# Attention with relative shift and sign MLP on one core: values of a unit in one block, a new table of jobs, and the output product summed in PSUM under the transposed layers

## The chip, the core and the metric

The kernel runs on one core of a Trainium2 chip. A time is the device time of one execution in microseconds (us); lower is better. All matrix engines, vector engines and queues named below belong to that one core: PE (TensorE), DVE (VectorE), ACT (ScalarE), POOL (GpSimd) and the DMA queue that SP (SyncE) feeds.

## What is computed

The input x is 16 batches of 512 rows of 128 numbers, float32. With xn the layernorm of x:

```
out = x + attention(xn) + mlp(xn)

attention:  y = layernorm(xn) * g + b
            q, k, v = y @ Wq + bq, y @ Wk + bk, y @ Wv + bv     # 16 heads of 8
            p = pe @ Wp                                         # positions, 512 rows
            s = (q + u) . k  +  relative_shift((q + v_bias) . p)
            head = softmax(s / sqrt(8)) @ v
            return head @ Wo + bo

mlp:        h = [xn, -xn];  h = relu(s0 * h @ sign(k0)) * 2
            h = relu(s1 * h @ sign(k1)) * 2;  return s2 * h @ sign(k2)   # 512, 512, 128 wide
```

The relative shift is done by writing a unit's 512x512 position scores to memory with rows of 513 and reading them back with rows of 512.

## The kernel before

**Units and halves.** A unit is one head of one batch: 256 units in all, numbered u. The program is written out as a list of halves (`HALVES`), two to a unit, 32 to a batch, and every engine's part walks through the same halves in the same order. In a half PE does, in this order:

1. two blocks of position scores (`positions`, L838, into the two banks of `ps_pos`) and two blocks of content scores (`content`, L850, into the two banks of `ps_con`), interleaved; the content of a unit comes `2*CONTENT_LAG` = 12 halves after its positions;
2. `turn` (L862): eight 128x128 transposes of finished scores into the two banks of `ps_pt`, 17 halves after the unit's positions;
3. the half's entry in the table of jobs, if it has one (`do_job`); all jobs share one bank, `ps_job`;
4. `values` (L876): products of the exponentials of half a unit with v (and a column of ones), into `ps_av`, eight matmuls in the program and 16 on the engine (two passes each), one half after their transposes.

**The other engines in a half.** ACT copies the positions to `pos_sb` (L509), takes the exponential of the transposed scores into `pt_sb` (L523), and then evicts the job (L478 to L495). DVE adds shifted positions to contents and takes the row maximum (L682, twice), subtracts it (L690, twice, with its own job between the two), and evicts the jobs V, TO, WO and TY. POOL splits evicted layers into a high and a low part in place (L397, L401 for q and k, L413, L416 for the MLP and the layernormed rows), four instructions a split. SP issues a write of 1 MB (L331) and a read of 1 MB (L341) for each unit: the write when its four position blocks lie in `pos_sb`, the read right behind the write that is two units later.

**Who waits for whom.** Content block 0 or 1 of a half needs its bank of `ps_con` free, which is the L682 of the half before. `turn` needs `ps_pt` free, which is the exponential of the half before. A job needs the job before it evicted from `ps_job`. `values` needs its exponential. The exponential overwrites `pt_sb`, which has four rows of 512 (`N_PT`), so it waits for the values one half back.

**The table.** `FRONT`, `MIDDLE` and `BACK` give each batch's jobs as (half, name, number): half 0 of a batch is where the positions of its first unit start, negative halves lie in the batch before, and numbers over 31 in the one after; `EARLY` and `END` are the same for the first and the last batch. A batch has T1, TZ (transposes of the two normalised inputs), QG and KG (four groups each of q and k), V, L0 and L1 (four blocks each of the first two layers), L2, TO (transposes of four groups of head outputs), TH (transposes of the assembled heads), WO (the output product, `w_sb["o"]` as weights, 512 rows at once) and TY (four transposes of the sum `y_t` of layers and attention). L1 and L2 have eight matmuls and are spread over two halves, four in each.

## Time and profile before

| | us |
|---|---|
| median of 3 runs | 1446.93 |
| lowest and highest of them | 1445.94, 1519.36 |
| the profiled execution | 1446.42 |
| its span in the trace | 1444.6 |

| engine | busy in the span |
|---|---|
| PE | 1434.1 us, 99% |
| DVE | 1337.1 us, 93% |
| ACT | 1226.2 us, 85% |
| POOL | 858.2 us, 59% |
| DMA, mean of 16 engines | 97.2% by the main queue, 381 GB/s |

Busy time of PE is modelled and includes the flight of a matmul through the array, so it overstates how near PE is to its peak. The granted TensorE clock is 0.9 or more of full speed in every slice of the span.

### The profile page before, as it was taken

The page shows a single profiled execution, that of the slowest core. Times are in us where ns is not written, and L with a number is a line of the kernel's source. Part 1 is how long each engine was busy: PE and PEld are TensorE (multiplying, and loading weights), DVE is VectorE, ACT ScalarE, POOL GpSimd, SP SyncE. Part 2 cuts the span into 40 slices and gives each one's busy share as a digit, 9 for nine tenths or more (in the row PEclk, how much of TensorE's full clock was granted, in tenths as well). Part 3 has the DMA queues.
Part 4 walks back from the last instruction along what each step waited for, and adds up shares of the span by engine and source line. Part 5 has one row for each costly group of instructions (what it writes and reads, how often), then busy time and mean ns, then how long its engine had stood idle before and what let it go on. Part 6 is the DMA issues. An engine that isn't in the chain of part 4 may idle for free.

```text
span 1444.6 us, 42221 instructions
## 1 busy us (share of the span) xinstructions
PE 1434.1 (99%) x16170; PEld 972.3 (67%) x16170; DVE 1337.1 (93%) x3489; ACT 1226.2 (85%) x1365; POOL 858.2 (59%) x1321
## 2 busy tenths in 40 slices
PE   8999999999999999999999999999999999999999
PEld 4666666666676666666666676666766666676666
DVE  6799999999999999999999999999999999999996
ACT  5688888888888898898888888888888888888874
POOL 5676565666665676565765666566565766654510
PEclk9999999999999999999999999999999999999999
DMA  5999999999999999999999999999999999999992
GB/s 202 356 403 409 392 402 390 387 401 383 408 388 390 396 380 408 386 397 395 383 411 378 408 385 391 401 386 405 382 393 402 386 400 390 398 382 392 394 398 105
DMA packets 80872, 550.45 MB, mean 381 GB/s; under 512 B 9376, under 2 KB 10528, under 8 KB 15136
## 3 DMA queue, kind: packets, MB, share of 16 engines
q1 hardware_dynamic: 80240, 547.06, 97.2%
q8 instruction: 129, 2.11, 0.6%
q10 hardware_dynamic: 432, 0.69, 0.2%
q14 instruction: 71, 0.58, 0.1%
HBM read 274.57 MB, written 273.15 MB: 379 GB/s over the span
## 4 chain that ended last, share of the span: by engine, by line
PE 96%; DVE 1%; DMA 1%; ACT 1%; issue 0%; POOL 0%; SPq 0%; POOLq 0%
PE ps_pt L862 36%; PE ps_av L876 19%; PE ps_pos L838 15%; PE ps_job L765 12%; PE ps_job L729 4%; PE ps_job L719 3%; PE ps_job L744 2%; PE ps_job L752 1%; PE ps_job L740 1%; PE ps_job L735 1%; DMA sc_sb<-shift 1%; PE ps_con L850 1%; ACT pt_sb L523 1%; DVE sc_sb L682 0%; PE ps_job L746 0%; PE ps_job L748 0%
## 5 line engine op out<-in xcount | busy, mean ns | idle before, releaser
L682 DVE CUSTOM_DVE_ANT_0 sc_sb<-ps_con,sc_sb 128x512 f32<-128x512 f32 x1024 | 662.0, 682 | 76.7 <-PE ps_con L850 68.2
L509 ACT COPY pos_sb<-ps_pos 128x1024 f32<-128x1024 f32 x510 | 518.3, 1016 | 177.9 <-PE ps_pos L838 170.9
L690 DVE TENSOR_SCALAR sc_sb<-sc_sb,nmax 128x512 f32<-128x512 f32 x1024 | 611.6, 629 | 0.1
L862 PE MATMUL ps_pt<-c_sb,sc_sb 128*128 128x128 f32 x4048 | 553.5, 280 | 1.8 <-ACT pt_sb L523 0.7
L523 ACT ACTIVATE pt_sb<-ps_pt 128x1024 f32<-128x1024 f32 x506 | 519.2, 1026 | 13.3 <-PE ps_pt L862 13.3
L862 PEld LDWEIGHTS ps_pt<-c_sb,sc_sb 128*128 128x128 f32 x4048 | 433.9, 141 | 126.6 <-issue 99.4
L876 PE MATMUL ps_av<-pt_sb,v_sb 128*9 128x128 f32 x8192 | 319.9, 274 | 0.1
L876 PEld LDWEIGHTS ps_av<-pt_sb,v_sb 128*9 128x9 f32 x8192 | 172.7, 90 | 184.3 <-issue 182.1
L413 POOL CAST h<-act_sb 128x256 fp32r<-128x256 f32 x256 | 97.6, 410 | 303.8 <-ACT act_sb L492 296.4
L850 PE MATMUL ps_con<-k_stack,q_stack 26*128 26x512 f32 x1024 | 261.1, 496 | 1.1 <-DVE nmax L682 1.0
L838 PE MATMUL ps_pos<-p_stack,q_stack 26*128 26x512 f32 x1024 | 259.8, 496 | 1.0 <-ACT pos_sb L509 0.7
L416 POOL TENSOR_TENSOR h<-act_sb,h 128x256 fp32r<-128x256 f32 x256 | 201.0, 806 | 0.0
L765 PE MATMUL ps_job<-h,w 128*128 128x512 f32 x640 | 189.6, 418 | 0.0
L838 PEld LDWEIGHTS ps_pos<-p_stack,q_stack 26*128 26x128 f32 x1024 | 97.2, 181 | 116.7 <-issue 111.7
L397 POOL TENSOR_TENSOR k_stack<-act_sb,c_sb 128x256 fp32r<-128x256 f32 x126 | 75.0, 616 | 100.0 <-ACT act_sb L487 96.3
L765 PEld LDWEIGHTS ps_job<-h,w 128*128 128x128 f32 x640 | 109.1, 190 | 15.1 <-issue 0.2
L397 POOL TENSOR_TENSOR q_stack<-act_sb,c_sb 128x256 fp32r<-128x256 f32 x124 | 73.4, 612 | 51.3 <-ACT act_sb L487 43.2
L401 POOL TENSOR_TENSOR q_stack<-act_sb,q_stack 128x256 fp32r<-128x256 f32 x124 | 102.1, 844 | 0.0
L850 PEld LDWEIGHTS ps_con<-k_stack,q_stack 26*128 26x128 f32 x1024 | 97.9, 181 | 5.4 <-DVE nmax L682 4.2
L401 POOL TENSOR_TENSOR k_stack<-act_sb,k_stack 128x256 fp32r<-128x256 f32 x126 | 101.2, 824 | 0.0
L492 ACT ACTIVATE act_sb<-ps_job,col 128x512 f32<-128x512 f32 x128 | 87.7, 685 | 0.6 <-PE ps_job L765 0.5
L682 DVE DVE_READ_ACCUMULATOR2_ANT nmax<- 128x1 f32 x1024 | 81.9, 80 | 0.0
(116 smaller groups left out, 1024.1 us busy)
## 6 DMA issues: line engine op xcount, KB each, us to landing
shift<-pos_sb SPq DMA_DIRECT2D x256, 1026.0 KB, 8.2
sc_sb<-shift SPq DMA_DIRECT2D x256, 1024.0 KB, 10.2
x_sb<-in_x SPq DMA_DIRECT2D x16, 256.0 KB, 10.6
out<-x_sb SPq DMA_DIRECT2D x15, 256.0 KB, 10.6
c_sb<-in_consts ACTq DMA_DIRECT2D x1, 288.0 KB, 7.4
sc_sb<-in_wp SPq DMA_DIRECT2D x1, 256.0 KB, 4.3
sc_sb<-in_stack_w ACTq DMA_DIRECT2D x1, 256.0 KB, 5.2
heads<-in_pe_t SPq DMA_DIRECT2D x1, 256.0 KB, 6.3
```

Of the source, the lines that this page charges most:

```text
L397: pool.tensor_tensor(dst[:, cut], src[:, cut], low.broadcast_to([P, S // len(CUTS)]), ALU.mult) \
L401: last = pool.tensor_tensor(dst[:, cut], src[:, cut], dst[:, cut].bitcast(F32), ALU.subtract)
L416: last = pool.tensor_tensor(dst[:, 1, cut], src[:, cut], dst[:, 0, cut].bitcast(F32), ALU.subtract)
L509: act.copy(to, ps_pos[:, :, :]).then_inc(s_pe, 1)
L523: act.activation(pt_sb[:, 2 * i:2 * i + 2, :], pt_banks(k)[:, :, :], ACT.Exp, scale=-1.0) \
L682: dve.tensor_tensor_reduce(sc_sb[:, m % N_SC, t, :], ps_con[:, k, :], sc_sb[:, m % N_SC, t, :], -SCALE, 3.4e38, ALU.add, ALU.min, nmax[:, ...
L690: dve.tensor_scalar(sc_sb[:, m % N_SC, t, :], sc_sb[:, m % N_SC, t, :], nmax[:, m % N_SC, t:t + 1], None, ALU.subtract).then_inc(s_sub, 1)
L765: return pe.matmul(ps_job[:, :], lhs, src[:, a, hl, :], start=(a == 0 and hl == 0), stop=(a == len(before) - 1 and hl == 1))
L838: ins = pe.matmul(ps_pos[:, bank, :], QS[rows, g, t * P:(t + 1) * P], PS[rows, g, :], start=True, stop=True)
L850: pe.matmul(ps_con[:, bank, :], QS[rows, g, t * P:(t + 1) * P], KS[rows, g, :], start=True, stop=True).then_inc(s_con, 1)
L862: last = pe.transpose(pt_banks(k)[:, j % 2, t * P:(t + 1) * P], sc_sb[:, u % N_SC, t, j * P:(j + 1) * P], id_sb)
L876: last = pe.matmul(ps_av[32 * t:32 * t + DH + 1, h % 4, :], v_sb[:, b % 2, j, h, :], pt_sb[:, j, t * P:(t + 1) * P], start=(j == 0), stop= ...
```

## The change

Three things are changed together.

**Values in pairs.** In all but the last 11 calls, `values` is called for both halves of a unit at once (32 matmul passes) in every second half, the odd ones, and not at all in the even ones. For this `pt_sb` has six rows (`N_PT`) in three pairs that are used in turn (`pt_half`), and the exponential waits for the values two calls back in place of one.

**The table.** Jobs have other halves. L1 and L2 issue six of their eight matmuls in their first half and two in their second (`LONG`). The layernorm statistics (`STATS`), which DVE takes in three halves, move from 50 to 44 halves ahead of their batch.

**The output product.** WO is no job any more. TY now issues, for each of its four 128-column blocks, the transpose of `y_t` without closing the sum, and on top of it a 128x128 matmul with a block of the transposed heads `o_t` as weights and `w_sb["o"]` as the moving operand. DVE's addition for WO goes. The last batch keeps its own form (`last_rows`).

To make room, the part of SBUF that is kept for descriptors of POOL's own DMA queue is 8192 in place of its default.

```
-    N_PT = 4
+    N_PT = 6
...
+                 (7, "PG", 3), (8, "L0", 3), (9, "QG", 2), (11, "KG", 2), (12, "L1", 0, 2), (14, "QG", 3),
+                 (16, "L1", 1, 2))
...
-        MIDDLE = ((12, "L1", 0, 2), (14, "KG", 3), (15, "QG", 3), (17, "L1", 1, 2), (20, "L1", 2, 2),
-                  (24, "L1", 3, 2), (36, "L2", 0, 2), (38, "TO", 0), (40, "TO", 1))
+        FRONT = ((-15, "T1", 0), (-11, "TZ", 0), (-7, "L0", 0), (-6, "QG", 0), (-4, "KG", 0), (-3, "L0", 1), (-1, "L0", 2),
+                 (0, "KG", 1), (4, "QG", 1), (6, "V", 0), (7, "L0", 3), (8, "QG", 2), (10, "L1", 0, 2), (12, "L1", 1, 2),
+                 (14, "QG", 3), (16, "KG", 2))
+        MIDDLE = ((18, "L1", 2, 2), (20, "KG", 3), (22, "L1", 3, 2), (34, "L2", 0, 2), (37, "TO", 0), (41, "TO", 1))
+        LONG = 6
-        BACK = ((51, "TO", 2), (54, "TO", 3), (60, "TH", 0), (62, "WO", 0), (64, "TY", 0))
+        BACK = ((47, "TO", 2), (56, "TO", 3), (59, "TH", 0), (62, "TY", 0))
...
-        STATS, NORM_X, NORM_Z = -50, -41, -27
+        STATS, NORM_X, NORM_Z = -44, -41, -27
...
+        SINGLE = 2 * UNITS - 11
...
-            return [k - 1 for k in turned(h) if k] + [2 * UNITS - 1] * (h == TURN_AT[-1] + 1)
+            pairs = [v for k in turned(h) if 0 < k < SINGLE and k % 2 == 0 for v in (k - 2, k - 1)]
+            return pairs + [k - 1 for k in turned(h) if k >= SINGLE] + [2 * UNITS - 1] * (h == TURN_AT[-1] + 1)
...
+        def pt_half(k):
+
+            k = 2 * (k % (N_PT // 2))
+            return pt_sb[:, k:k + 2, :]
...
-                    wait(act, s_av, k - 1)
-                    act.activation(pt_sb[:, 2 * i:2 * i + 2, :], pt_banks(k)[:, :, :], ACT.Exp, scale=-1.0) \
+                    wait(act, s_av, k - 2)
+                    act.activation(pt_half(k), pt_banks(k)[:, :, :], ACT.Exp, scale=-1.0) \
...
-                elif name == "WO":
-                    last = dve.tensor_tensor(y_t[:, :], ps_job[:, :], y_t[:, :], ALU.add)
...
-                            return pe.transpose(dst, y_t[:, cut], id_sb)
+                            pe.matmul(dst, y_t[:, cut], id_sb, is_transpose=True, start=True, stop=False)
+                            return pe.matmul(dst, o_t[:, cut], w_sb["o"], start=False, stop=True)
...
-                first, end = (-(-len(todo) * i // many) for i in (part, part + 1))
+                first, end = (0, len(todo)) if many == 1 else ((0, LONG), (LONG, len(todo)))[part]
...
-                for k in products[:1]:
+                for k in products[:2 if products and products[0] < SINGLE - 1 else 1]:
```

On PE, two halves of the first batch boundary stand like this in the kernel before. L838 and L850 are positions and contents, L862 the transposes of `turn`, L746 the job TH, L765 the job L0, L876 the values:

```order
L862 MATMUL ps_pt<-c_sb,sc_sb 128x128 x8
L746 MATMUL ps_job<-c_sb,heads 128x128 x4
L876 MATMUL ps_av<-pt_sb,v_sb 9x128 x8
L838 MATMUL ps_pos<-p_stack,q_stack 128x512
L850 MATMUL ps_con<-k_stack,q_stack 128x512
L838 MATMUL ps_pos<-p_stack,q_stack 128x512
L850 MATMUL ps_con<-k_stack,q_stack 128x512
L862 MATMUL ps_pt<-c_sb,sc_sb 128x128 x8
L765 MATMUL ps_job<-x_t,w 128x512 x2
L876 MATMUL ps_av<-pt_sb,v_sb 9x128 x8
```

The same place in the changed kernel, where positions, contents and `turn` are L845, L857 and L869, TH is L752, the job KG is L737 and the values are L883:

```order
L869 MATMUL ps_pt<-c_sb,sc_sb 128x128 x8
L752 MATMUL ps_job<-c_sb,heads 128x128 x4
L883 MATMUL ps_av<-pt_sb,v_sb 9x128 x16
L845 MATMUL ps_pos<-p_stack,q_stack 128x512
L857 MATMUL ps_con<-k_stack,q_stack 128x512
L845 MATMUL ps_pos<-p_stack,q_stack 128x512
L857 MATMUL ps_con<-k_stack,q_stack 128x512
L869 MATMUL ps_pt<-c_sb,sc_sb 128x128 x8
L737 MATMUL ps_job<-z_t,wk 128x512
L845 MATMUL ps_pos<-p_stack,q_stack 128x512
```

The half of TH now holds the values of a whole unit, and the half after it holds KG and goes from the job straight to the next positions.

On PE, the job TY of the changed kernel (L754 the transposes of `y_t`, L755 the products with `w_sb["o"]`, a part of c_sb; `o_t` is a view of z_sb):

```order
L869 MATMUL ps_pt<-c_sb,sc_sb 128x128 x8
L754 MATMUL ps_job<-c_sb,y_t 128x128
L755 MATMUL ps_job<-c_sb,z_sb 128x128
L754 MATMUL ps_job<-c_sb,y_t 128x128
L755 MATMUL ps_job<-c_sb,z_sb 128x128
L754 MATMUL ps_job<-c_sb,y_t 128x128
L755 MATMUL ps_job<-c_sb,z_sb 128x128
L754 MATMUL ps_job<-c_sb,y_t 128x128
L755 MATMUL ps_job<-c_sb,z_sb 128x128
L845 MATMUL ps_pos<-p_stack,q_stack 128x512
```

Before, these were one matmul `L735 MATMUL ps_job<-z_sb,c_sb 128x512` (WO) in one half and four transposes (TY) two halves later. They now stand in one half without values.

On DVE, the end of a batch before the change (L605 is the addition for WO, L608 that for TY):

```order
L690 TENSOR_SCALAR sc_sb<-sc_sb,nmax 128x512
L605 TENSOR_TENSOR y_t<-ps_job,y_t 128x512
L690 TENSOR_SCALAR sc_sb<-sc_sb,nmax 128x512
L682 ISA sc_sb,nmax<-ps_con,sc_sb 128x512
L682 ISA nmax 128x1
L682 ISA sc_sb,nmax<-ps_con,sc_sb 128x512
L682 ISA nmax 128x1
L690 TENSOR_SCALAR sc_sb<-sc_sb,nmax 128x512 x2
L682 ISA sc_sb,nmax<-ps_con,sc_sb 128x512
```

And after it (L616 is the addition for TY):

```order
L698 TENSOR_SCALAR sc_sb<-sc_sb,nmax 128x512
L616 TENSOR_TENSOR x_sb<-ps_job,x_sb 128x512
L698 TENSOR_SCALAR sc_sb<-sc_sb,nmax 128x512
L690 ISA sc_sb,nmax<-ps_con,sc_sb 128x512
L690 ISA nmax 128x1
```

The addition of WO is gone, and the one of TY stands two halves earlier.

## Rows read from the trace of the kernel before

**Rows 1.** The page's parts 1 and 4: busy time by engine; the chain's engines
```profile
PE 1434.1 (99%) x16170; PEld 972.3 (67%) x16170; DVE 1337.1 (93%) x3489; ACT 1226.2 (85%) x1365; POOL 858.2 (59%) x1321
PE 96%; DVE 1%; DMA 1%; ACT 1%; issue 0%; POOL 0%; SPq 0%; POOLq 0%
```

**Rows 2.** Busy time in a stretch of one batch
```profile
100.00:187.15 87.15, 87.15 (x1009) 59.45 (x1008) 82.44 (x216) 76.32 (x86) 55.24 (x85) 1.00 1.01 400
```

**Rows 3.** PE's waits in the whole span: total, times, longest
```profile
PE ps_con L850 <- DVE nmax L682: 1.0, 2, 0.8
```

**Rows 4.** Chain of work in order of time, 703 to 716 us: start, length, what
```profile
703.97 1.03 PE ps_pt L862 x8
704.99 0.44 PE ps_job L748 x4
705.43 0.55 PE ps_av L876 x16
...
707.45 0.86 PE ps_job L729 x2
...
710.32 0.69 PE ps_job L719 x3
...
715.52 0.93 PE ps_job L765 x4
```

**Rows 5.** The same chain at the jobs V and WO
```profile
775.85 0.89 PE ps_job L740 x8
...
786.40 0.86 PE ps_job L735 x2
```

**Rows 6.** Timeline of PE: start, first start to last end, count
```profile
40.55 0.63 PE L707 MATMUL ps_av<-w 128*128 128x512 f32 x2
41.12 0.50 PE L838 MATMUL ps_pos<-p_stack,q_stack 26*128 26x512 f32 x1
...
703.47 0.49 PE L838 MATMUL ps_pos<-p_stack,q_stack 26*128 26x512 f32 x1
...
704.83 0.60 PE L748 MATMUL ps_job<-c_sb,y_t 128*128 128x128 f32 x4
705.36 0.62 PE L876 MATMUL ps_av<-pt_sb,v_sb 128*9 128x128 f32 x16
705.91 0.50 PE L838 MATMUL ps_pos<-p_stack,q_stack 26*128 26x512 f32 x1
...
706.36 1.09 PE L862 MATMUL ps_pt<-c_sb,sc_sb 128*128 128x128 f32 x8
```

**Rows 7.** The page's groups of the values and of DVE's subtraction
```profile
L690 DVE TENSOR_SCALAR sc_sb<-sc_sb,nmax 128x512 f32<-128x512 f32 x1024 | 611.6, 629 | 0.1
...
L876 PE MATMUL ps_av<-pt_sb,v_sb 128*9 128x128 f32 x8192 | 319.9, 274 | 0.1
```

**Rows 8.** Timeline of ACT
```profile
705.03 1.02 ACT L523 ACTIVATE pt_sb<-ps_pt 128x1024 f32<-128x1024 f32 x1
```

**Rows 9.** Timeline of DVE
```profile
704.00 0.69 DVE L682 CUSTOM_DVE_ANT_0 sc_sb<-ps_con,sc_sb 128x512 f32<-128x512 f32 x1 [0.76 <-PE ps_con L850]
...
706.91 0.68 DVE L682 CUSTOM_DVE_ANT_0 sc_sb<-ps_con,sc_sb 128x512 f32<-128x512 f32 x1
...
708.13 0.87 DVE L690 TENSOR_SCALAR sc_sb<-sc_sb,nmax 128x512 f32<-128x512 f32 x2
708.93 0.69 DVE L675 COPY o_sb<-ps_av 128x512 f32<-128x512 f32 x1
...
713.35 1.85 DVE L690 TENSOR_SCALAR sc_sb<-sc_sb,nmax 128x512 f32<-128x512 f32 x2
```

**Rows 10.** Timeline of POOL
```profile
713.31 1.61 POOL L401 TENSOR_TENSOR q_stack<-act_sb,q_stack 128x256 fp32r<-128x256 f32 x2
```

**Rows 11.** Main DMA queue (packets, MB, share); reads (KB, us to landing); DVE's waits
```profile
q1 hardware_dynamic: 80240, 547.06, 97.2%
...
sc_sb<-shift SPq DMA_DIRECT2D x256, 1024.0 KB, 10.2
...
DVE sc_sb L682 <- DMA sc_sb<-shift: 4.8, 2, 3.4
```

More of the change, by code:

```diff
@@ L182, in attention_mlp @@
                  (2, "QG", 1), (3, "KG", 0), (3, "L0", 0), (4, "L0", 1), (4, "PG", 2), (5, "V", 0), (6, "L0", 2), (7, "KG", 1),
-                 (7, "PG", 3), (8, "L0", 3), (9, "QG", 2), (11, "KG", 2))
-        FRONT = ((-16, "T1", 0), (-9, "TZ", 0), (-6, "V", 0), (-5, "QG", 0), (-3, "L0", 0), (-1, "KG", 0),
-                 (1, "KG", 1), (2, "QG", 1), (3, "L0", 1), (7, "L0", 2), (9, "QG", 2), (10, "KG", 2), (11, "L0", 3))
-        MIDDLE = ((12, "L1", 0, 2), (14, "KG", 3), (15, "QG", 3), (17, "L1", 1, 2), (20, "L1", 2, 2),
-                  (24, "L1", 3, 2), (36, "L2", 0, 2), (38, "TO", 0), (40, "TO", 1))
+                 (7, "PG", 3), (8, "L0", 3), (9, "QG", 2), (11, "KG", 2), (12, "L1", 0, 2), (14, "QG", 3),
[5 more added lines that the diff above has]
+        LONG = 6
         WARM = {h: {0: 4, 14: 6}.get(h, 1 if 3 <= h < 10 else 2) for h in range(18)}
-        BACK = ((51, "TO", 2), (54, "TO", 3), (60, "TH", 0), (62, "WO", 0), (64, "TY", 0))
+        BACK = ((47, "TO", 2), (56, "TO", 3), (59, "TH", 0), (62, "TY", 0))
         END = ((45, "TO", 1), (46, "TO", 2), (48, "TO", 3), (49, "LAST", 0))
@@ L380, in norm @@
                 if k == 1 and b >= 3:
-                    pool.wait_ge(s_job, job("WO", b - 3))
+                    pool.wait_ge(s_job, job("TY", b - 3))
                 scale_rows(pool, b, k)
@@ L449, in take_job @@
                 k = job(name, b, c)
-                if name in ("V", "TO", "WO", "TY"):
+                if name in ("V", "TO", "TY"):
                     return
@@ L580, in take_job @@
                     return
-                if name not in ("V", "TO", "WO", "TY"):
+                if name not in ("V", "TO", "TY"):
                     return
@@ L733, in job_parts @@
                                               start=True, stop=True)]
-                if name == "WO":
-                    return [lambda: pe.matmul(ps_job[:, :], w_sb["o"], o_t[:, :], start=True, stop=True)]
                 if name in ("T1", "TZ", "V", "TO", "TH", "TY"):
@@ L876, in values @@
                         last = pe.matmul(ps_av[32 * t:32 * t + DH + 1, h % 4, :], v_sb[:, b % 2, j, h, :],
-                                         pt_sb[:, j, t * P:(t + 1) * P], start=(j == 0), stop=(j == NT - 1))
+                                         pt_half(2 * u + i)[:, j % 2, t * P:(t + 1) * P],
+                                         start=(j == 0), stop=(j == NT - 1))
                 last.then_inc(s_av, 1)
@@ L964 @@
     }
-    nc = bacc.Bacc("TRN2", target_bir_lowering=False, num_devices=1)
+    nc = bacc.Bacc("TRN2", target_bir_lowering=False, num_devices=1, dynamic_dma_scratch_size=8192)
     arrays, args = {}, []
```

## The prediction

> **What bounds the kernel now.** I read the page's shares first: PE is busy 99% of the span and makes 96% of the chain that ends last [rows 1]. The stretch of one batch says the same: in 87.15 us PE is busy 87.15, DVE 82.44, ACT 76.32, POOL 55.24 [rows 2]. Busy PE could still hide waits, so I looked at what PE waited for: on DVE's reduction twice in the whole span, 1.0 us together [rows 3]. So each half costs what PE's own instructions cost, and the chain in order of time gives the parts: turn 1.03, a job of four transposes 0.44, values 0.55, KG 0.86, QG 0.69, four MLP products 0.93 (0.23 each), all [rows 4]; V 0.89 and WO 0.86 [rows 5]. The half with TY runs from 703.47 to 705.91 [rows 6], 2.44 us, so a half without a job is 2.00: turn 1.02, values 0.55, and the 0.43 left is positions and contents.
>
> **Pairs on PE.** What pairing removes is the change of kind of matmul. One values block lasts 0.62 on the timeline and a pass 0.274, so its 16 passes start within 0.35; the next kind starts 0.07 before the modelled end [rows 6, 7], which is 0.55 from start to start. The 16 passes run as four groups of four, so 0.35 is three steps of about 0.11, and 16 passes more cost four steps, 0.44. A pair is then 0.55 + 0.44 = 0.99 in place of 1.10: **0.11 to 0.12 saved per unit**. This holds if going from a job straight to positions costs no more than from a job to values. The trace has such a place in batch 0: L707 with 512 columns starts at 40.55, lasts 0.63, and L838 starts at 41.12, 0.06 before its end; from a job to values it is 0.07 (704.83 + 0.60 against 705.36) [rows 6]. So no extra. 16 units: 16 x 0.12 = 1.9 us per batch.
>
> **TY on PE.** WO's 0.86 goes, TY grows by four 128x128 float32 products. V is exactly four of these: 0.89 [rows 5]. Cost 0.03 per batch. Mixing them with transposes might cost a step each; from below they could be hidden behind the transposes' weight loads. I take 0.03, with 0 to 0.4 as ends. The Trainium skill (TensorE: Matmul & The Clock Gate, Back-to-back issue gap) gives about 81 ns per 128-column matmul in a stream; the eight passes of V show 0.89/8 = 111 ns, so the trace does not agree. By the page's figure, an estimate, the products would cost 0.65 and TY would gain 0.2 a batch; I go by the trace.
>
> PE's own sum for a batch: 87.15 - 1.9 + 0.03 = 85.3. Times 15 batches that is 28 us, if nothing else comes to wait. DVE loses WO's addition, one instruction like the 0.69 copy [rows 9], so its load is 81.8 of 85.3: no longer far from the bound, and that is the question.
>
> **What the uneven halves do.** With pairs, even halves are 1.45 + job and odd ones 2.44 + job. From the table: even halves with TO 1.89, QG 2.14 (four), KG 2.31 (four), V 2.34, TY with its products 2.78, six MLP products 2.85 (five); odd halves 2.44 without a job (one), 2.88 with four transposes (six) and 2.91 with two products (nine). The mean is right, but two things need a length of their own.
>
> *ACT.* The exponential of a half frees `ps_pt` for the next turn. It starts at 705.03 and ends at 706.05, the next turn starts at 706.36 [rows 6, 8], in a half of 2.44; so a half can be no shorter than 2.44 - 0.31 = 2.13, plus some hundredths for the signal. TO at half 24 (1.89) loses about 0.25, the four QG lose 0.03 each: **0.35 per batch**. Other halves are free of it: their exponential is over before.
>
> *DVE.* When DVE has waited, its first reduction starts 0.53 after the half's first matmul (704.00 against 703.47) [rows 6, 9]; the second reduction ends 0.61 + 0.68 later and frees the bank that the next half's second content needs. So DVE may lag by the half's length less 1.85: 0.3 us in a QG half, 0.45 in a KG half, 1.0 in a long one. DVE's own length is 2.02 for a bare half (706.91 to 708.93), about 0.6 more with a task, and more when POOL works: two subtractions take 0.87 alone and 1.85 while POOL splits q [rows 9, 10]. Over the run L690 is busy 611.6 us against 1024 x 0.435 = 445 [rows 7, 9]: 166 us lost, 10.4 a batch, 0.58 for each of its 18 splits. The Trainium skill (SBUF — State Buffer, Who interferes with whom) states that such an instruction and one of POOL exclude each other for a whole instruction; by that rule, the rows agree (0.98 us more for two subtractions).
>
> I carried DVE's lag through the 32 halves: lag + 2.02 + 0.6 if the half has a task (TO 0.5) + 0.58 if the half before has a split job - the half's length, never below zero, and PE waits for what exceeds the room. With the new table the room is exceeded at halves 16, 23, 25, 27 and 28, by 0.9 us in sum. The same carry with the old table gives 0.5 at halves 16 to 18 and 23, where the whole trace has 1.0 us in two waits [rows 3]; so the carry is too harsh by that, and I charge **0.45 per batch**. The ends: 0 (with 0.3 for a split) and 2.3 (with 0.75).
>
> **What costs nothing.** Evictions: the shortest gap from a job's end to the next job is after an even half, positions and turn 1.45, and ACT's or DVE's eviction takes 0.7; if ACT lags by one eviction this cover is nearly gone, which adds up to 0.3 a batch at the worst. The third pair of `pt_sb` makes the exponential's wait for values as loose as it was. POOL has the same splits, and 30 us of room. The read of a unit is issued about 1.7 us into half 7 after its positions start and needed in half 12, five halves later: 5 x 2.7 - 1.7 = 11.9 against 10.2 us to land, and DVE waited for it only 4.8 us in all [rows 11]. Those five halves are three odd and two even ones, which are longer than their mean, so room is kept. The size of the descriptor area concerns POOL's own queue, on which nothing is issued. Values of V's batch begin 12 halves after V. The transposed heads are evicted two halves before TY.
>
> **Sum.** 1.9 - 0.03 - 0.35 - 0.45 = 1.1 us a batch. 15 batches: 16 us; batch 0 has seven pairs and is not bound by PE alone, the last batch has halves without jobs where the short half runs into ACT's floor: 0 to 1 us together. The profiled execution had 1446.42, so 1430; the median is 0.5 above it. I predict **1430 us**, 1.1% less.
>
> **The rivals.**
> 1. *All waits hidden.* If POOL's work falls mostly beside DVE's idle time, only the floor at TO stays: 1.6 a batch, 1422; without that too, 1419. For it: DVE's lag in the old table never made PE wait. Against: the even halves leave a third of the old room. 0.14, of which half ends below 1418, since a cheaper change of kind or a cheaper TY is needed for more than 2%.
> 2. *DVE takes the place.* With the harsh end, 2.3 + 0.35 a batch waits against 1.87 saved: 1447 + 15 x 0.8 = 1459; with waits of 1.8 no change, 1447. For it: DVE's load is 96% of the new batch, and six jobs with splits stand close from half 25 to 31. Against: the same carry overstates the waits of before. 0.16 (mostly 1440 to 1450).
> 3. *Pairs save nothing, or the way from a job to positions is dearer.* If a pair costs twice 0.55, the waits of 0.8 remain alone: 1447 + 12 = 1459. This is slower, decided by one number, the 0.99 of a pair. Against: the four steps are visible. 0.05.
> 4. *Reads come late.* If the landing of reads grows from 10.2 to over 12 us because transfers are asked for 1% faster, each unit's first reduction waits: 1 us a unit is 256 us at the far end, a tenth of it 25 us: 1455. Decided at 11.9 us. For it: the main queue is busy 97.2% [rows 11]. 0.05.
> My forecast, 1420 to 1440, has 0.60.
>
> A measurement of this kernel can tell about 2% from no change, so the bounds are 1418 and 1476: faster 0.10, same 0.87, slower 0.03. The range that leaves a tenth on each side is 1419 to 1448.
>
> **What would show it.** Positions start to start of 2.31 in KG halves and 2.88 in odd halves with transposes; the paired values 0.99 on the chain; TY with products 1.33. PE's waits: turn on the exponential, near 0.25 x 15 at TO; contents on L682's successor, 0.2 to 0.9 a batch, in halves 16 and 23 to 28. DVE's busy time less by 10 us. If contents wait more than 1.8 us a batch, rival 2; if reads are named among DVE's waits with tens of us, rival 4; if a paired block is 1.1, rival 3.

## The result and the profile after

| | before | after |
|---|---|---|
| median | 1447.01 us | 1439.62 us |
| lowest | 1444.55 us | 1436.73 us |
| profiled execution, its span | 1446.42, 1444.6 us | 1441.53, 1439.7 us |
| one batch, from trace | 87.15 us | 86.70 us |

The ratio is 0.995 with a 95% interval of 0.9936 to 0.9964: faster by half a per cent, clear of noise, but less than half of the 1.1% forecast. PE's work shrank as forecast; three quarters of it came back as waits. Single executions of several of these kernels, that of before among them (1519.36 us is its highest), take 3 to 8% longer than the others of the same kernel and are left out of every ratio.

The page's part 1 and 4 of the changed kernel, beside [rows 1]:

```profile
PE 1419.0 (99%) x16260; PEld 1013.5 (70%) x16260; DVE 1318.2 (92%) x3474; ACT 1210.4 (84%) x1365; POOL 853.8 (59%) x1321
PE 88%; DVE 8%; issue 3%; DMA 1%; ACT 1%; SPq 0%; ACTq 0%
```

PE's share of the chain fell from 96 to 88%, and DVE's rose from 1 to 8%: DVE now ends waits of PE. (The page also puts the waits of `turn` down to DVE; below they turn out to be for ACT, so the 8% says too much.) The length of a batch is read from the job TH, which comes once in each (timeline of PE: start, length, count), and the same stretch as [rows 2] now holds idle time of PE:

```profile
689.75 0.60 PE L752 MATMUL ps_job<-c_sb,heads 128*128 128x128 f32 x4
...
776.45 0.60 PE L752 MATMUL ps_job<-c_sb,heads 128*128 128x128 f32 x4
```

```profile
100.00:187.15 87.15, 86.57 (x1026) 62.28 (x1016) 81.91 (x215) 75.75 (x86) 55.04 (x85) 1.00 1.01 395
```

776.45 - 689.75 = 86.70 us. All stretches from one TH to the next take this within 0.01 but the last one, so each half can be laid beside the forecast. Of the 32 halves, 25 have the length that PE's work alone gives, to 0.04 us; seven are longer (the half meant is the one in the table of jobs, counted within the batch):

| half | its work by the forecast | measured | what PE waits for |
|---|---|---|---|
| 0 | 2.31 | 2.39 | DVE's reduction (`ps_con`), for the next content |
| 3 | 2.91 | 3.40 | DVE's reduction |
| 5, 9, 15 | 2.88 | 3.00, 3.00, 3.01 | exponential of the QG half before |
| 25 | 2.91 | 3.29 | exponential of the TO half before |
| 27 | 2.88 | 3.02 | both at once |

The excess is 0.08 + 0.49 + 0.37 + 0.38 + 0.14 = 1.46 us (halves 5, 9 and 15 together are the 0.37). The forecast's work of 85.3 and these 1.4 to 1.5 make the 86.70. The forecast's own lengths of halves add to 84.97 and not to its 85.3; the 0.3 between them is the 0.01 to 0.04 by which most halves are longer than listed.

**The wait for the exponential.** Timeline of PE, halves 24 to 27 (positions L845, turn L869, values L883):

```profile
680.91 0.49 PE L845 MATMUL ps_pos<-p_stack,q_stack 26*128 26x512 f32 x1
...
682.81 0.50 PE L845 MATMUL ps_pos<-p_stack,q_stack 26*128 26x512 f32 x1
...
683.65 1.06 PE L869 MATMUL ps_pt<-c_sb,sc_sb 128*128 128x128 f32 x8 [0.34 <-DVE sc_sb L698]
684.47 0.71 PE L772 MATMUL ps_job<-x_t,w 128*128 128x512 f32 x2
685.11 1.06 PE L883 MATMUL ps_av<-pt_sb,v_sb 128*9 128x128 f32 x32
686.10 0.50 PE L845 MATMUL ps_pos<-p_stack,q_stack 26*128 26x512 f32 x1
```

And ACT at the same time:

```profile
681.48 1.02 ACT L519 COPY pos_sb<-ps_pos 128x1024 f32<-128x1024 f32 x1 [0.33 <-PE ps_pos L845]
682.48 1.02 ACT L533 ACTIVATE pt_sb<-ps_pt 128x1024 f32<-128x1024 f32 x1
```

Half 24 lasts 1.90 (680.91 to 682.81), so turn 25 is due at 682.81 + 0.44 = 683.25. The exponential ends at 683.50 and the turn starts at 683.65, 0.14 to 0.15 later (the releaser named in brackets is DVE's subtraction, which has a signal of its own on which `turn` waits too; the one that turn 25 needs, the first of half 23, had ended at 680.84, and run 9 below removes this wait with DVE as it was). The signal's way is part of the floor: a half in front of such a turn is no shorter, in effect, than 2.27 us. The values pair lasts 0.99 (685.11 to 686.10), as forecast.

**The wait for DVE.** Timeline of DVE in halves 30 and 31, then in 1 and 2:

```profile
698.29 0.48 DVE L698 TENSOR_SCALAR sc_sb<-sc_sb,nmax 128x512 f32<-128x512 f32 x1
699.41 0.69 DVE L616 TENSOR_TENSOR x_sb<-ps_job,x_sb 128x512 f32<-128x512 f32 x1 [0.64 <-PE ps_job L755]
700.02 1.01 DVE L698 TENSOR_SCALAR sc_sb<-sc_sb,nmax 128x512 f32<-128x512 f32 x1
700.96 0.68 DVE L690 CUSTOM_DVE_ANT_0 sc_sb<-ps_con,sc_sb 128x512 f32<-128x512 f32 x1
```

```profile
619.98 1.89 DVE L698 TENSOR_SCALAR sc_sb<-sc_sb,nmax 128x512 f32<-128x512 f32 x2
621.79 0.68 DVE L683 COPY o_sb<-ps_av 128x512 f32<-128x512 f32 x1
622.39 0.68 DVE L690 CUSTOM_DVE_ANT_0 sc_sb<-ps_con,sc_sb 128x512 f32<-128x512 f32 x1
...
623.00 0.68 DVE L690 CUSTOM_DVE_ANT_0 sc_sb<-ps_con,sc_sb 128x512 f32<-128x512 f32 x1
```

PE in half 3, and POOL:

```profile
623.25 0.50 PE L845 MATMUL ps_pos<-p_stack,q_stack 26*128 26x512 f32 x1
623.74 0.50 PE L857 MATMUL ps_con<-k_stack,q_stack 26*128 26x512 f32 x1
```

```profile
619.99 1.60 POOL L411 TENSOR_TENSOR k_stack<-act_sb,k_stack 128x256 fp32r<-128x256 f32 x2
```

DVE reaches its addition for TY at once after the first subtraction and stands 0.64 us idle, because TY now lasts 1.4 us on PE. Its queue is in order: the second subtraction and the next half's reductions stand behind. That second subtraction also meets POOL and takes 1.01 in place of 0.48. So DVE enters half 31 at 1.65 us after the half's first matmul (700.96 against 699.31), where 0.53 is the least. The long half 31 takes most of this away again, PE waits 0.08 for it in half 0, and in half 1 the reductions start at 0.84, which is only 0.31 above the least. There POOL's split of k stretches the two subtractions to 1.89 (1017 and 952 ns), and a copy stands ahead of the reductions of half 2, which start at 2.03; the second of them ends at 623.68 and holds content 2 of half 3 back to 623.74, 0.49 late. DVE's waits show the new one, and no such wait stood among those of before:

```profile
DVE sc_sb L690 <- PE ps_con L857: 76.1, 163, 2.9
DVE x_sb L616 <- PE ps_job L755: 9.6, 15, 0.7
DVE sc_sb L690 <- DMA sc_sb<-shift: 5.7, 2, 3.3
```

9.6 us in 15 times is one wait of 0.64 a batch. The DMA row is as in [rows 11].

### The profile page after: what moved, and what is told of

Its sections match the earlier page's. It is cut to its first block, busy times and chain, and to the rows that moved or that the text cites. A ratio compares the mean times of both kernels' runs of the same rounds, so it can differ in the third digit from the quotient of the medians.

```text
span 1439.7 us, 42385 instructions
## 1 busy us (share of the span) xinstructions
PE 1419.0 (99%) x16260; PEld 1013.5 (70%) x16260; DVE 1318.2 (92%) x3474; ACT 1210.4 (84%) x1365; POOL 853.8 (59%) x1321
## 3 DMA queue, kind: packets, MB, share of 16 engines
q8 instruction: 130, 2.13, 0.6%
## 4 chain that ended last, share of the span: by engine, by line
PE 88%; DVE 8%; issue 3%; DMA 1%; ACT 1%; SPq 0%; ACTq 0%
PE ps_pt L869 32%; PE ps_av L883 18%; PE ps_pos L845 13%; PE ps_job L772 12%; DVE sc_sb L698 4%; PE ps_job L737 4%; DVE sc_sb L690 3%; PE ps_job L750 1%; PE ps_con L857 1%; PE ps_job L746 1%; PE ps_job L759 1%; PE ps_job L755 1%; PE ps_job L727 1%; DMA sc_sb<-shift 1%; PE ps_av L715 1%
## 5 line engine op out<-in xcount | busy, mean ns | idle before, releaser
L690 DVE CUSTOM_DVE_ANT_0 sc_sb<-ps_con,sc_sb 128x512 f32<-128x512 f32 x1024 | 662.6, 683 | 86.3 <-PE ps_con L857 76.1
L519 ACT COPY pos_sb<-ps_pos 128x1024 f32<-128x1024 f32 x510 | 518.7, 1017 | 177.1 <-PE ps_pos L845 175.3
L698 DVE TENSOR_SCALAR sc_sb<-sc_sb,nmax 128x512 f32<-128x512 f32 x1024 | 593.1, 612 | 0.1
L869 PE MATMUL ps_pt<-c_sb,sc_sb 128*128 128x128 f32 x4048 | 551.5, 279 | 9.7 <-DVE sc_sb L698 5.8
L869 PEld LDWEIGHTS ps_pt<-c_sb,sc_sb 128*128 128x128 f32 x4048 | 434.0, 141 | 136.2 <-issue 91.2
L857 PE MATMUL ps_con<-k_stack,q_stack 26*128 26x512 f32 x1024 | 271.2, 496 | 2.0 <-DVE nmax L690 1.7
L883 PE MATMUL ps_av<-pt_sb,v_sb 128*9 128x128 f32 x8192 | 272.9, 273 | 0.1
L845 PE MATMUL ps_pos<-p_stack,q_stack 26*128 26x512 f32 x1024 | 259.3, 495 | 1.3 <-ACT pos_sb L519 0.7
L883 PEld LDWEIGHTS ps_av<-pt_sb,v_sb 128*9 128x9 f32 x8192 | 197.6, 90 | 71.6 <-issue 71.2
L845 PEld LDWEIGHTS ps_pos<-p_stack,q_stack 26*128 26x128 f32 x1024 | 97.1, 181 | 166.4 <-issue 110.3
L426 POOL TENSOR_TENSOR h<-act_sb,h 128x256 fp32r<-128x256 f32 x256 | 187.2, 752 | 0.0
L411 POOL TENSOR_TENSOR q_stack<-act_sb,q_stack 128x256 fp32r<-128x256 f32 x124 | 111.4, 917 | 0.0
L857 PEld LDWEIGHTS ps_con<-k_stack,q_stack 26*128 26x128 f32 x1024 | 103.4, 181 | 11.1 <-DVE nmax L690 9.7
L411 POOL TENSOR_TENSOR k_stack<-act_sb,k_stack 128x256 fp32r<-128x256 f32 x126 | 104.5, 849 | 0.0
## 6 DMA issues: line engine op xcount, KB each, us to landing
sc_sb<-shift SPq DMA_DIRECT2D x256, 1024.0 KB, 10.7
```

The costliest lines, as they stand in the source:

```text
L411: last = pool.tensor_tensor(dst[:, cut], src[:, cut], dst[:, cut].bitcast(F32), ALU.subtract)
L426: last = pool.tensor_tensor(dst[:, 1, cut], src[:, cut], dst[:, 0, cut].bitcast(F32), ALU.subtract)
L519: act.copy(to, ps_pos[:, :, :]).then_inc(s_pe, 1)
L690: dve.tensor_tensor_reduce(sc_sb[:, m % N_SC, t, :], ps_con[:, k, :], sc_sb[:, m % N_SC, t, :], -SCALE, 3.4e38, ALU.add, ALU.min, nmax[:, ...
L698: dve.tensor_scalar(sc_sb[:, m % N_SC, t, :], sc_sb[:, m % N_SC, t, :], nmax[:, m % N_SC, t:t + 1], None, ALU.subtract).then_inc(s_sub, 1)
L845: ins = pe.matmul(ps_pos[:, bank, :], QS[rows, g, t * P:(t + 1) * P], PS[rows, g, :], start=True, stop=True)
```

## The experiments

Each kernel was timed beside the kernel before. Batch lengths come from the trace as above.

| run | ratio to before (95%) or one time | batch, us |
|---|---|---|
| changed kernel | 0.995 (0.9936 to 0.9964) | 86.70 |
| 1 pairs only | 1.0054 (1.0035 to 1.0073) | 87.7 |
| 2 product in TY only | 1.0033 (1.0021 to 1.0045) | 87.44 |
| 3 changed, no pairs | 1.003 (1.002 to 1.004) | 87.38 |
| 4 half 24 unpaired | 0.9963 (0.995 to 0.9976) | 86.74 |
| 5 short exponential | 1524.95 us, with late reads | 85.77 before these |
| 6 less POOL | 1432.57 us | 86.13 |
| 7 both | 1420.73 us | 85.43 |
| 8 TY's addition late | 0.9912 (0.9895 to 0.9928) | 86.12 |
| 9 exponential in two | 0.9942 (0.992 to 0.9964) | 86.44 |
| 10 both 8 and 9 | 0.9897 (0.9878 to 0.9915) | 85.86 |
| 11 as 5, once more | 1522.64 us, with late reads; 1426.95 us | 85.77 before these |
| 12 as 10, TO and L0 swapped | 1425.65, 1429.0 us | 85.87 |

### 1. Pairs alone

The new values order and `pt_half` on the old table, with WO. Two of the lines; the rest (`pt_half`, the wait on the values two calls back, the descriptor area) is as in the change.

```
-    N_PT = 4
+    N_PT = 6
...
-            return [k - 1 for k in turned(h) if k] + ...
+            pairs = [v for k in turned(h) if 0 < k < SINGLE and k % 2 == 0 for v in (k - 2, k - 1)]
```

> The kernel before with the values in pairs and nothing else: old table, WO a job. Theory (a half can be no shorter than 2.27 us, since the turn starts 0.14 us after the exponential of the half before has ended): even halves of the old table with four transposes are 1.89 by PE's work (TY, TO, TO, T1, TO, TH: six), QG 2.14 (one), so PE waits 6 x 0.38 + 0.13 = 2.4 a batch, against 1.9 saved, and the room for DVE's lag in those halves is under 0.1, which costs 0.5 to 2 more: 88.2 to 89.7 us a batch, 1462 to 1485. Rival (DVE's lag alone makes the waits, the floor is 2.13): 1.5 less from the floor, 86.7 to 88.2 a batch, 1440 to 1462. Rival (pairs save nothing): 89.5 to 91.5, over 1482.

Measured 1453.36 us and 87.66 to 87.74 a batch, slower than before. The range of the theory began at 88.2; its floor part fits to some hundredths and its DVE part did not come. The total alone lies in the range of the rival (floor 2.13, all waits DVE's), so it is the single turns that decide. 87.15 - 1.9 + 6 x 0.38 + 0.12 = 87.7. In the half after half 8 (1.89 of work) the turn is late by 0.4 (timeline of PE, positions L846, turn L870):

```profile
622.36 0.49 PE L846 MATMUL ps_pos<-p_stack,q_stack 26*128 26x512 f32 x1
...
623.20 1.06 PE L870 MATMUL ps_pt<-c_sb,sc_sb 128*128 128x128 f32 x8 [0.33 <-ACT pt_sb L531]
```

0.84 after the positions in place of 0.44, in all six such places, and each time 0.14 to 0.15 after the exponential's end. So pairs need a table that puts the short jobs into the halves with values, and DVE's lag cost nothing here (in half 29 a content is 0.23 late, but the turn behind it waits longer still).

### 2. The product in TY alone

```
-                            return pe.transpose(dst, y_t[:, cut], id_sb)
+                            pe.matmul(dst, y_t[:, cut], id_sb, is_transpose=True, start=True, stop=False)
+                            return pe.matmul(dst, o_t[:, cut], w_sb["o"], start=False, stop=True)
...
-        BACK = (..., (60, "TH", 0), (62, "WO", 0), (64, "TY", 0))
+        BACK = (..., (60, "TH", 0), (64, "TY", 0))
```

> The kernel before with WO's product put into TY and nothing else. Theory: the products cost PE 0.03 us a batch more than WO did, and DVE has one task less: 87.15 to 87.25 a batch, 1446 to 1449. Rival (mixing transposes and products costs a step each, 0.4 a batch): 1453.

1450.23 us, 87.44 a batch: 0.29 more, where 0.03 was expected. The half with TY grew to 3.34 (2.45 + 0.89), so the products cost what V costs, and mixing them with transposes costs nothing that shows. The rival's time (1453) was above the measured one, and its step a block (0.4 in this half) is not there. The other 0.25 is in the half after the one that WO left empty. Exponential, then turn:

```profile
698.50 1.02 ACT L523 ACTIVATE pt_sb<-ps_pt 128x1024 f32<-128x1024 f32 x1
```

```profile
698.95 0.49 PE L839 MATMUL ps_pos<-p_stack,q_stack 26*128 26x512 f32 x1
...
699.67 1.07 PE L863 MATMUL ps_pt<-c_sb,sc_sb 128*128 128x128 f32 x8 [0.22 <-ACT pt_sb L523]
```

The empty half lasts 2.01, the exponential ends at 699.52, and the turn comes 0.15 later, at 0.72 in place of 0.44 after its positions. It is the same floor of 2.27, in the old table without pairs. So the forecast of this run, which priced PE's instructions alone, missed what its empty half would do: taking work out of a half that is already short gives nothing.

### 3. The changed kernel without pairs

```
-        SINGLE = 2 * UNITS - 11
+        SINGLE = 0
...
-                for k in products[:2 if products and products[0] < SINGLE - 1 else 1]:
+                for k in products[:1]:
```

> The changed kernel with the values of one half at a time, as before: new table, products in TY, six and two MLP products kept. Theory: no half is then under 2.0, the one without a job (half 1), where PE waits 0.27 for the exponential; TY's half is 3.34; everything else has room. PE 87.18 + 0.27 + a little for DVE where L2 and TO crowd: 87.4 to 87.8 a batch, 1449 to 1456. So pairs are worth 0.7 to 1.1 a batch in the new table. Rival (the new table itself costs DVE waits of over 1 us): above 88.3, 1465.

1450.14 us, 87.38 a batch: at the lower edge of what was expected. The half after the empty half 1 is 0.2 longer than its work, where 0.27 was expected; the rest has no wait. Exponential of half 1 and turn of half 2 (positions at 624.27):

```profile
623.82 1.03 ACT L533 ACTIVATE pt_sb<-ps_pt 128x1024 f32<-128x1024 f32 x1
```

```profile
624.90 1.09 PE L869 MATMUL ps_pt<-c_sb,sc_sb 128*128 128x128 f32 x8
```

Here the turn starts 0.05 after the exponential's end and not 0.14. It is in an even half, where `turn` waits for the exponential alone; in the odd halves, where all the changed kernel's waits for the exponential lie, it waits for a subtraction as well.

Table and product without pairs are slower than before, pairs without them too; only together do they gain. In this table pairs are worth 0.68 a batch of their 1.9.

### 4. Half 24 unpaired

One unit in sixteen has its first values in half 24, its second in half 25.

```
+            solo = (24,)
-            pairs = [v for k in turned(h) if 0 < k < SINGLE and k % 2 == 0 for v in (k - 2, k - 1)]
+            pairs = [v for k in turned(h) if 0 < k < SINGLE
+                     for v in ((k - 1,) * (h % 32 in solo) if k % 2 else
+                               (k - 2, k - 1)[1 if (h - 1) % 32 in solo and TURN_AT[k - 1] == h - 1 else 0:])]
```

> The changed kernel with one unit in sixteen not paired, that of half 24, the shortest half (TO alone, 1.89). Theory of the floor at 2.27: half 24 becomes 2.44, half 25 2.47, together 4.91 in place of 5.19; PE's work grows by 0.12 and 0.37 of waiting goes: 86.42 a batch in place of 86.70, 4 us less in all, 1435 to 1437. Rival (the wait in half 25 is for DVE's lag): it stays, and the time rises by up to 0.12 a batch, 1440 to 1442.

1440.44 us, 86.74 a batch: no gain. Halves 24 and 25 came out as the floor says (2.46 and 2.48, no wait), but half 27 grew from 3.02 to 3.29. There the second content (L860) is 0.41 late:

```profile
687.41 0.49 PE L848 MATMUL ps_pos<-p_stack,q_stack 26*128 26x512 f32 x1
687.82 0.50 PE L860 MATMUL ps_con<-k_stack,q_stack 26*128 26x512 f32 x1
```

So both theories hold in part: the exponential is what PE waits for in half 25, and that wait gave DVE the time to catch up. Take it away, and DVE's lag, which the forecast's carry had put at halves 25, 27 and 28, shows in its place.

### 5 and 11. ACT relieved

Half of the exponentials is left out; the rest of `pt_sb` is filled with zeros once, ahead of the work.

```
-                    act.activation(pt_half(k), pt_banks(k)[:, :, :], ACT.Exp, scale=-1.0) \
+                    act.activation(pt_half(k)[:, 0, :], pt_banks(k)[:, 0, :], ACT.Exp, scale=-1.0) \
```

> The changed kernel with the exponential taken of one of the two banks of ps_pt only (the other half of the exponentials is left out, so the attention is not the reference's). ACT is then free 0.45 us earlier in each half and the floor falls to about 1.8. Theory: the waits of halves 5, 9 and 15 (3 x 0.12) go; those of 25 (0.37) and 27 (0.14) are taken over by DVE's lag in half 27, as leaving half 24 unpaired showed (0.41 there): 86.3 to 86.45 us a batch against 86.70. Rival (the exponential holds them all): 85.8.

> The kernel with one bank of exponentials only, once more (half of the exponentials is left out), because from its fifth batch on the first run showed reads that landed 14 us after their issue and DVE waiting for them, 121 us in all, while its third and fourth batch took 85.77. Theory (ACT's time alone sets the floor, and the late reads have nothing to do with the change): batches of 85.77 throughout where reads land in under 11 us, waits of 0.33 in half 27 and none in 3, 5, 9, 15; about 1425 if no disturbance comes. Rival (a shorter batch asks more of the DMA engines than they give): reads late again from the fifth batch on, over 1500.

In both traces of this kernel reads land late from the fifth or sixth batch on (the medians are 14.0 and 13.7 us in place of 10.7), and DVE waits 121 us for them. Only the batches before that are read here. They took 85.77, against 86.3 to 86.45 expected and 85.8 for the rival. Halves 5, 9 and 15 lost their 0.12, half 25 its 0.38, and half 27 grew to 3.21 where 3.29 was expected; half 0 kept its 0.08; but half 3 lost its 0.49 as well. So the rival's total came, and not by the exponential holding all: runs 6 and 8 take the wait of half 3 away with the exponential whole.

What happened to half 3 is in DVE's subtractions. DVE still stands for TY here and enters half 31 at 1.66 and half 0 at 1.03 (0.91 in the changed kernel). But in halves 0 and 1 the four subtractions take 476, 474, 487 and 951 ns, where the changed kernel has 785, 475, 1017 and 952. So the reductions start at 0.64 in half 1 and at 1.30 in half 2, in place of 0.84 and 2.03. In half 1 the first of them starts 1.86 after the half's first matmul and POOL's second step at 2.02; in the changed kernel it is 2.06 and 2.07. That step was not foreseen: POOL's splits begin when ACT has evicted, so a shift of some tenths of a microsecond in ACT moves them against DVE.

The other execution of run 11, without a trace, took 1426.95, near the 1425 expected where no read is late. Whether a shorter batch makes late reads likelier is open: two of three executions had them, and this was not tested further.

### 6. POOL relieved

The edit stands in the splits of q and k, 8 of the 18 in a batch. The low parts of the other ten (L426 in the changed kernel) are whole, though what was expected says every split.

```
+                        cut = slice(cut.start, cut.start + 8)
                         last = pool.tensor_tensor(dst[:, cut], src[:, cut], dst[:, cut].bitcast(F32), ALU.subtract)
```

> The changed kernel with POOL's low parts (second half of every split) taken of 8 of 256 columns only; the rest of the low parts is left out, so the result is less exact or wrong. POOL then rarely works beside DVE's subtractions. Theory: DVE's lag waits go (half 3 0.49, half 0 0.07) and the floor stays (0.37 + 4 x 0.12): 86.1 to 86.2 us a batch. Rival (the waits in half 3 are for something else, a DMA or an eviction): 86.6 to 86.7.

86.13 a batch (86.1 to 86.2 expected): half 3 is 2.92 and half 0 is 2.32, without a wait, and halves 5, 9, 15, 25 and 27 keep theirs to 0.01. The half microsecond in half 3 needs POOL beside DVE: the subtractions of half 1 take 475 and 473 ns here. TY still sets when DVE's addition starts in half 30, but the subtraction behind it takes 0.48 in place of 1.01, and half 31 is entered at 1.11.

### 7. Both relieved

The edits of 5 and 6 together.

> Both of these: one bank of exponentials only, and POOL's low parts on 8 of 256 columns. Theory: no wait is left, PE's own work is the batch, 85.3 us. Rival (something third holds PE): over 85.6.

TH to TH in this kernel:

```profile
338.00 0.27 PE L754 MATMUL ps_job<-c_sb,heads 128*128 128x128 f32 x1
...
423.42 0.27 PE L754 MATMUL ps_job<-c_sb,heads 128*128 128x128 f32 x1
```

85.42 (85.43 in most batches), with 0.10 of it still a wait for DVE in half 27. The forecast's sum for PE's own work, 85.3, is confirmed: no third resource holds PE, and the changed kernel's 86.70 is these 85.3 and 1.4 of the two waits.

### 8. TY's addition behind the second subtraction

```
-                    if k == 0:
-                        for j in taken(h):
-                            take_job(*j)
+                    for j in taken(h):
+                        if (k == 1) == (j[0] == "TY"):
+                            take_job(*j)
```

> The changed kernel with DVE's addition for TY behind the second subtraction of its half in place of between the two. DVE stands idle 0.64 us there in each batch, waiting for the long TY. Theory: its lag at half 31 falls from 1.65 by about 0.4 and that carries through halves 0 to 2 into the wait of 0.49 in half 3: 86.3 to 86.45 a batch, 1434 to 1436. Rival (PE's waits clip the lag on the way, and half 3 is made by POOL in half 1 alone): 86.65 to 86.7, 1439.

1433.22 us, 86.12 a batch, 0.58 less than the changed kernel: the whole wait of half 3 and that of half 0. DVE at the end of half 30, and entering 31 (positions of PE at 608.21):

```profile
607.19 1.01 DVE L698 TENSOR_SCALAR sc_sb<-sc_sb,nmax 128x512 f32<-128x512 f32 x2
608.31 0.69 DVE L616 TENSOR_TENSOR x_sb<-ps_job,x_sb 128x512 f32<-128x512 f32 x1
608.92 0.68 DVE L690 CUSTOM_DVE_ANT_0 sc_sb<-ps_con,sc_sb 128x512 f32<-128x512 f32 x1
```

The reductions of half 31 start 0.71 after the positions in place of 1.65: more than the 0.4 expected, since the second subtraction meets POOL only for a part (617 ns in place of 1015). Among DVE's waits there is none for the job TY any more.

How this reaches half 3 is less direct than was expected. In half 1 the reductions start at 0.71 in place of 0.84, only 0.13 earlier. The rest comes from POOL. The two subtractions of half 1:

```profile
615.37 1.35 DVE L698 TENSOR_SCALAR sc_sb<-sc_sb,nmax 128x512 f32<-128x512 f32 x2
```

They take 480 and 952 ns in place of 1017 and 952: starting 0.13 earlier, the first one escapes the split. Of the 0.67 by which the reductions of half 2 start earlier (1.36 and not 2.03), 0.54 is this and 0.13 is the lag itself. So neither run 6 nor run 8 takes away one cause alone (in 6, half 31 was entered earlier too), and run 5 has DVE's full stand for TY and no wait in half 3. What the wait needs is that both subtractions of half 1 meet POOL; the stand for TY is one of the things that put them there.

### 9, 10 and 12. The exponential in two instructions

In the five short halves (4, 8, 14, 24, 26) each bank's exponential has its own signal, and the next turn's first four transposes wait for the first alone.

```
+                    if k in CUT_EXP:
+                        act.activation(pt_half(k)[:, 0, :], pt_banks(k)[:, 0, :], ACT.Exp, scale=-1.0) \
+                           .then_inc(s_cut, 1)
+                        act.activation(pt_half(k)[:, 1, :], pt_banks(k)[:, 1, :], ACT.Exp, scale=-1.0) \
+                           .then_inc(s_exp, 1)
...
+                    if cut and j % 2:
+                        pe.wait_ge(s_exp, k)
```

> The changed kernel with the exponential of the five short even halves of a batch (4, 8, 14, 24, 26) taken in two instructions, one for each bank, each with its own signal, so that the first four transposes of the next turn wait for the first alone. Result as before. Theory: the floor of 2.27 falls by about 0.4 there; halves 5, 9 and 15 lose their 0.12 each; the waits at 25 and 27 pass to DVE's lag, as in the other runs: 86.35 us a batch, 1434. Rival (the second instruction costs ACT so much that copies come late): 86.7 or more.

1436.29 us, 86.44 a batch (86.35 expected): halves 5, 9 and 15 are 2.89, half 25 is 3.01, half 27 is 3.29. The turn of half 25 starts 0.43 after its positions, with the subtractions of half 24 where they were (the first ends 0.81 into half 25): it was the exponential that the turn waited for, and not DVE.

> The same with DVE's addition for TY behind the second subtraction. Theory: both gains add if they lie in different stretches (halves 5 to 27, and 31 to 3): 86.0 us a batch, 1429 to 1431. Rival (TY's place is worth nothing): as the run before.

1430.34 us, 85.86 a batch. The gains of 8 (0.58) and 9 (0.26) add to 0.84: they lie in different stretches. It is the fastest of the kernels that have a ratio, 1.0% under before. ACT in one short half, by its timeline:

```profile
595.34 0.60 ACT L537 ACTIVATE pt_sb<-ps_pt 128x512 f32<-128x512 f32 x1
595.83 0.59 ACT L539 ACTIVATE pt_sb<-ps_pt 128x512 f32<-128x512 f32 x1
596.31 0.69 ACT L500 ACTIVATE act_sb<-ps_job,c_sb 128x512 f32<-128x512 f32 x1
```

Two instructions take 0.97 from start to the next start, one takes 0.92: the split costs 0.05.

The last edit moves TO of the fourth group to half 25 and L0's first block to half 24.

```
-        FRONT = (..., (-7, "L0", 0), ...
+        FRONT = (..., (-8, "L0", 0), ...
-        BACK = ((47, "TO", 2), (56, "TO", 3), ...
+        BACK = ((47, "TO", 2), (57, "TO", 3), ...
```

> Two-instruction exponentials in the short halves, TY's addition behind the second subtraction, and TO of group 3 in half 25, L0 of block 0 in half 24. What still waits in the run before is content in half 27 (0.41), for DVE's lag, which has TO in half 24 and a copy in 25. Theory: TO one half later does not change DVE's sum over halves 24 to 26, only POOL's place: the wait in half 27 stays between 0.2 and 0.5, 85.7 to 86.0 a batch, 1428 to 1432. Rival (the task in the shortest half is what makes the lag): half 27 has no wait, 85.45 a batch, 1424.

85.87 a batch, and 3.34 in half 27: moving the task did not take the wait away, as was expected if DVE's sum over halves 24 to 26 makes it; no run changes that sum alone. Two executions of four are left to compare, 1425.65 and 1429.0, and do not tell it from run 10 (1428.56 to 1431.01); of the difference in span, 1423.9 against 1429.2, 3.8 us are in the first batch, 77.9 against 81.7 us, which hold nearly the same jobs.

## Why the prediction was wrong

**PE's work: right.** Forecast 85.3 a batch, 85.4 with both waits out of the way (run 7). The pair at 0.99, the way from a job to positions at no extra cost and TY at V's price stand in the trace as written, the lengths of 25 halves to 0.04.

**The floor of a half: the mechanism right, the size wrong.** The step was "a half can be no shorter than 2.13, plus some hundredths for the signal". The hundredths are 0.14 to 0.15, in each of the five places where a steady batch waits for the exponential. The step named five halves; with 2.27 they lose 0.37 and four times 0.12, 0.85 a batch and not 0.35. No turn of a steady batch waited for its exponential before, and the one signal that the rows show, from the end of PE's content (703.47 + 0.50) to DVE's reduction (704.00), is 0.03; so "some hundredths" looked fair. But the trace of before has the figure, in its first batches. ACT's exponential and then PE's turn:

```profile
68.89 1.02 ACT L523 ACTIVATE pt_sb<-ps_pt 128x1024 f32<-128x1024 f32 x1
```

```profile
70.06 1.07 PE L862 MATMUL ps_pt<-c_sb,sc_sb 128*128 128x128 f32 x8 [0.22 <-DVE sc_sb L690]
```

From 69.91 to 70.06 it is 0.15. This is 0.5 of the 0.65 us by which a batch came out above the forecast.

**DVE's lag: the size nearly right by luck, the place wrong.** 0.45 was charged and 0.57 is there, but not in halves 16, 23, 25 and 28. In half 27 the lag is there and is covered by the wait for the exponential (run 4). The 0.45 itself does not hold: with the terms as stated (0.6 for V, TY, each copy and each of the three parts of the statistics) the carry gives 1.5 us for the new table and not 0.9, in halves 16, 22 to 25, 27 and 28, though it gives the 0.5 of the old one. The text does not list the tasks by half, so the difference cannot be followed further; a sum too small stood for waits that mostly did not come.

What shows is half 3, and two steps missed it. The carry took 0.58 for every split, its mean, and, as stated, compared the lag with the room before it added the half's copy; in half 1 the split takes 1.0 and the copy stands ahead of the next reductions. And it priced TY's addition (0.6) without asking when DVE reaches the instruction and when PE is done, although TY had grown from 0.44 to 1.33 us: after the first subtraction, at about 0.53 + 1.22 + 0.4 = 2.15 us into the half, against 1.45 + 1.33 = 2.78. That subtraction of two numbers was to be had from the rows, and is the 0.64 of the trace. Moving the addition is worth 0.58 a batch by run 8, most of it by way of one subtraction that no longer meets POOL. A carry with means cannot foresee such a meeting; it hangs on 0.1 us.

DVE's busy time fell by 18.9 us and not by 10 (1337.1 to 1318.2), since its subtractions met POOL less: their busy time went from 611.6 to 593.1.

**Outside the steady batches.** The forecast gave 0 to 1 us of gain. The first batch took 82.40 in place of 81.04 and began 0.44 later. Runs 9, 10 and 12, whose first batches hold nearly the same jobs, took 77.98, 81.73 and 77.93; so it is not shown that this 1.4 us is a part of the change. Why the first batch is so unsteady stays open.

**The rivals.** The median, 1439.62, is at the slow end of the 1420 to 1440 that had 0.60. Rival 2 (DVE takes the place) points the same way, and four tenths of the waits are DVE's; but its waits of 1.8 a batch are 0.57. Rival 1 did not come. Rival 3 is refuted by the pair's 0.99, rival 4 by the rows of DMA; reads landed in 10.7 us in place of 10.2 and DVE waited for them 5.7 us in all.

## What to carry to other kernels

When work is moved so that steps become uneven, give each short step a floor: what the other engines must do in it, plus the way of the signal, measured and not guessed (the first batches of the old trace may have it); the step's saving ends at that floor. When a producer's job grows, find the instruction that consumes it and compare when each is ready, since an in-order engine that stands for it delays all that is queued behind. The price can then appear several steps later, where the delayed instructions meet another engine's. Where two waits lie close together, removing the one that shows tells little until the other is priced too.

## What the runs showed of the hardware

- From the end of ACT's exponential to the start of the transpose that waits for it: 0.14 to 0.15 us in odd halves, as in the changed kernel (683.50 to 683.65) and in run 2 (699.52 to 699.67), and 0.05 in even ones, as in run 3 (624.85 to 624.90). In the program the turn of an odd half waits for a subtraction of DVE first and then for the exponential, that of an even half for the exponential alone. That the second wait costs the 0.09, though the subtraction was long over, is not shown: no run removes it.
- A float32 transpose that opens a sum and a float32 matmul that closes it in the same bank run at the pace of each alone: the half with TY takes 2.79 us (half 30), where the common 1.45, four transposes at 0.44 and V's eight passes at 0.89 add to 2.78.
- A subtraction of DVE meets POOL's split or not depending on tenths of a microsecond: the same two instructions took 785 and 475 ns in half 0, 1017 and 952 in half 1, and 477 and 476 in half 2. The Trainium skill (SBUF — State Buffer, Who interferes with whom) says that the one that comes second waits for the other's whole instruction; run 6 agrees, in which the subtractions of half 1 took 475 and 473 ns with POOL's second step cut short, in place of 1017 and 952.
